# Cached values as one contiguous transfer, four keys in a row on a partition, and the turned probabilities with a stride of four

## The reference, cut to what matters

```python
q = _rope(_rmsnorm(q, q_norm_w), pos)
k = _rope(_rmsnorm(k, k_norm_w), pos)
kc = k_cache[block_table].reshape(bsz, L, HK, D)      # L = 512 cached keys
vc = v_cache[block_table].reshape(bsz, L, HK, D)
k_all = jnp.concatenate([kc, k], axis=1)              # 640 keys
v_all = jnp.concatenate([vc, v], axis=1)
...
scores = jnp.einsum('bqhd,bkhd->bhqk', q, k_all) * SCALE
scores = jnp.where(valid[:, None, None, :], scores, -1e+30)
probs = jax.nn.softmax(scores, axis=-1)
o = jnp.einsum('bhqk,bkhd->bqhd', probs, v_all)
return jnp.einsum('bse,de->bsd', o.reshape(bsz, seqlen, HQ * D), Wo)
```

## Time and profile before

| | us |
|---|---|
| median of 3 runs | 1304.53 (1304.43 to 1305.79) |
| the profiled execution, its own time | 1303.22 |
| its span, first to last instruction | 1301.4 |
| PE busy | 1252.7 (96%) |
| DVE busy | 984.4 (76%) |
| ACT busy | 835.0 (64%) |
| POOL busy | 830.8 (64%) |
| mean granted PE clock | 0.987 of full speed |

### The profile page before, as it was taken

How to read it: one execution, slowest core, us unless ns; L and a number is a source line. 1 busy time by engine, 2 the same in 40 slices (tenths; PEclk the granted TensorE clock), 3 DMA queues, 4 the chain that set the end, 5 groups by cost and what they waited for, 6 DMA issues and landing times. The chain is left out here.

```text
span 1301.4 us, 26180 instructions
## 1 busy us (share of the span) xinstructions
PE 1252.7 (96%) x7464; PEld 1067.8 (82%) x7464; DVE 984.4 (76%) x2380; ACT 835.0 (64%) x2501; POOL 830.8 (64%) x783
## 2 busy tenths in 40 slices
PE   5899998799999999999999999999999999999988
PEld 4666765588888888888888888888888888888878
DVE  3577757478878878888788788868888888888866
ACT  2677777466676666666766666666667666666731
POOL 1457557476767676668765876577667756775731
PEclk9899998899999999999999999999999999999999
DMA  8555553445555545555555555545555555555541
GB/s 288 214 200 205 203 211 130 111 117 139 137 139 141 140 133 149 131 140 141 151 130 141 138 140 128 144 126 139 131 140 143 137 142 142 135 138 137 137 130 66
DMA packets 288561, 191.48 MB, mean 147 GB/s; under 512 B 151201, under 2 KB 256674, under 8 KB 287266
## 3 DMA queue, kind: packets, MB, share of 16 engines
q1 hardware_dynamic: 287408, 189.64, 51.0%
q10 hardware_dynamic: 1010, 0.17, 0.1%
HBM read 143.60 MB, written 79.69 MB: 172 GB/s over the span
## 5 line engine op out<-in xcount | busy, mean ns | idle before, releaser
L1745 POOL TENSOR_TENSOR b_p_l<-b_moved,b_p_h 128x640 fp32r<-128x640 f32 x128 | 200.9, 1570 | 167.4 <-PE ps L1341 86.5
L1480 ACT ACTIVATE b_pf<-b_sm,b_mn 128x640 f32<-128x640 f32 x256 | 212.2, 829 | 128.0 <-DVE b_mn L1590 127.9
L1590 DVE CUSTOM_DVE_ANT_0 b_sm<-ps,mask_row,b_rstd 128x640 f32<-128x640 f32 x256 | 224.9, 878 | 51.8 <-PE ps L1267 46.5
L1492 ACT ACTIVATE b_p_h<-b_moved 128x640 fp32r<-128x640 f32 x128 | 94.6, 739 | 163.5 <-DMA b_moved<-blocks_of_probs 162.0
L1626 DVE SCALAR_TENSOR_TENSOR b_hacc<-ps,b_ri,b_hacc 128x512 f32<-128x512 f32 x248 | 182.4, 736 | 4.3 <-PE ps L1267 4.0
L1265 PE MATMUL ps<-b_w_h,x1t_h 128*128 128x512 f32 (+1 forms) x512 | 179.3, 350 | 0.1
L1265 PE MATMUL ps<-b_kt_h,b_qt_h 128*128 128x320 f32 x512 | 168.9, 330 | 6.0 <-DVE b_mn L1590 5.7
L1266 PE MATMUL ps<-b_w_l,x1t_h 128*128 128x512 f32 (+1 forms) x512 | 173.8, 340 | 0.0
L1267 PE MATMUL ps<-b_w_h,x1t_l 128*128 128x512 f32 (+1 forms) x512 | 173.6, 339 | 0.0
L1267 PE MATMUL ps<-b_kt_h,b_qt_l 128*128 128x320 f32 x512 | 158.9, 310 | 0.0
L1266 PE MATMUL ps<-b_kt_l,b_qt_h 128*128 128x320 f32 x512 | 158.7, 310 | 0.0
(11 more groups left out here) (170 smaller groups left out, 3344.6 us busy)
## 6 DMA issues: line engine op xcount, KB each, us to landing
blocks_of_probs<-b_blk SPq DMA_DIRECT2D x128, 320.0 KB, 2.5
b_moved<-blocks_of_probs SPq DMA_DIRECT2D x512, 80.0 KB, 2.0
kv_of_batch<-in_kv SPq DMA_DIRECT2D x128, 256.0 KB
b_ck<-kv_of_batch SPq DMA_DIRECT2D x64, 256.0 KB, 4.0
b_cv<-kv_of_batch SPq DMA_DIRECT2D x256, 64.0 KB, 1.9
raw<-in_w SPq DMA_DIRECT2D x32, 384.0 KB, 3.2
raw<-in_wo SPq DMA_DIRECT2D x32, 256.0 KB, 2.8
a_xt<-in_xt SPq DMA_DIRECT2D x8, 256.0 KB, 5.6
```

The lines of the kernel that those rows point to most:

```text
L1480: act.activation(pf[:, h % 2], sm[:, h % 2], ACT.Exp, bias=mn[:, m.b % 2, h:h + 1], scale=-1.0, accum_out=rs[:, m.b % 2, h:h + 1]).then_in ...
L1492: act.activation(blocks_of(p_h[:, :, h * P:(h + 1) * P]), moved[:, d].rearrange("p (a t j) -> p a t j", a=LT, j=QUAD), ACT.Copy).then_inc( ...
L1590: dve.tensor_tensor_reduce(sm[:, h % 2], score_row, mask_row[:, m.b], rstd[:, m.b % 4, h:h + 1], -MASKED, ALU.add, ALU.min, mn[:, m.b % 2, ...
L1745: pool.tensor_tensor(blocks_of(p_l[:, :, h * P:(h + 1) * P]), moved[:, d].rearrange("p (a t j) -> p a t j", a=LT, j=QUAD), blocks_of(p_h[: ...
```

## The change

The HBM buffer is laid out anew: for each sequence and head all keys of the 16 pages stand first and all values behind them, so that the 512 values of an item are one run of 256 KB. `value_rows` loads them in a single transfer: each partition takes four values in a row (2 KB), so partition p holds the keys 4p to 4p+3, key 4p+t in place t. Tile t of the values now has the keys t, t+4, t+8 and so on. The turned probabilities must follow. `turn_probs` loads as weights each fourth column of `pf` for the four tiles of cached keys, a step of 16 bytes in place of 4; the fifth tile, the new keys, stays as it was. `turn_blocks` becomes two instructions: one over the 512 cached columns, which reads with the same step, and one over the 128 new ones. ACT waits for 16 instead of 64 on the values' semaphore. The gather writes two runs of 16 KB for each head in place of one of 32 KB. Scores, mask, minima and exponents keep their order of keys.

```diff
@@ -83,7 +83,8 @@
                                                        min_val=0, max_val=PAGES - 1)
     for k in range(FOUR):
         n = first + k
-        sp.dma_start(kv_dram[n // NPP, :, n % NPP], t["kv"][bass.ds(four[k], 1)].rearrange("a g n -> (a g) n")).then_inc(gathered, 16)
+        page = t["kv"][bass.ds(four[k], 1)].rearrange("a g (k n) -> (a g) k n", k=2)
+        sp.dma_start(kv_dram[n // NPP, :, :, n % NPP], page).then_inc(gathered, 16)
 
 
 def phase1(nc, ctx, t, x1t_h, x1t_l, ident, consts, raw, raw_in, x1_dram, kv_dram, pages, gathered, ps):
@@ -1173,7 +1174,10 @@
             return ap.rearrange("p (c t j) -> p c t j", c=LT, j=QUAD)
 
         def by_tile(ap):
-            return ap.rearrange("p (t c j) -> p c t j", c=LT, j=QUAD)
+            return ap.rearrange("p (c j t) -> p c t j", c=LT, j=QUAD)
+
+        def by_rows(ap):
+            return ap.rearrange("p (c j) -> p c j", j=QUAD)
 
         def blocks_of(ap):
             return ap.rearrange("p t (a j) -> p a t j", a=LT)
@@ -1200,14 +1204,13 @@
                 if m.g == 0:
                     sp.wait_ge(gathered[m.b], 16 * NPP)
                 wait(sp, kcl_sb, m.n)
-                keys = kv_dram[m.b, m.g, :, 0:HD * PSIZE].rearrange("j (d s) -> d j s", d=HD)
+                keys = kv_dram[m.b, m.g, 0].rearrange("j (d s) -> d j s", d=HD)
                 sp.dma_start(ck[:].rearrange("p (j s) -> p j s", s=PSIZE), keys).then_inc(ck_in, 16)
             def value_rows(m):
 
                 wait(sp, vcl_sb, m.n)
-                for q in range(LT):
-                    rows_of = kv_dram[m.b, m.g, :, HD * PSIZE:].rearrange("(t q) (s d) -> q s t d", q=LT, d=HD)[q]
-                    sp.dma_start(cv[q * PSIZE:(q + 1) * PSIZE], rows_of).then_inc(cv_in, 16)
+                rows_of = kv_dram[m.b, m.g, 1].rearrange("j (p n) -> (j p) n", n=LT * HD)
+                sp.dma_start(cv[:].rearrange("p t d -> p (t d)"), rows_of).then_inc(cv_in, 16)
 
             def blocks_away(m, h):
 
@@ -1314,7 +1317,8 @@
                 pe.wait_ge(exp_sb, REP * m.n + h + 1)
                 wait(pe, pl_sb, len(BY_PE) * m.n + BY_PE.index(h))
                 for i in range(NT):
-                    mm = pe.transpose(turned_row[:, i], pf[:, h % 2, i * P:(i + 1) * P], ident[:])
+                    keys = pf[:, h % 2, L:] if i == LT else pf[:, h % 2, i:L:LT]
+                    mm = pe.transpose(turned_row[:, i], keys, ident[:])
                 mm.then_inc(pt_ps, 1)
 
             def value_pairs(m):
@@ -1457,7 +1461,7 @@
                 act.activation(kt_h[:, m.b % 2, L:], ps[:, PJK, 0:P], ACT.Copy).then_inc(knh_sb, 1)
 
             def cache_values(m):
-                act.wait_ge(cv_in, 16 * LT * (m.n + 1))
+                act.wait_ge(cv_in, 16 * (m.n + 1))
                 wait(act, pv_ps, m.n - 1)
                 act.activation(v_h[:, m.b % 2], cv[:], ACT.Copy).then_inc(vch_sb, 1)
 
@@ -1601,7 +1605,9 @@
                     dve.wait_ge(x1_out, 16 * B)
                 dve.wait_ge(exp_sb, REP * m.n + h + 1)
                 wait(dve, blk_out[d], 16 * m.n)
-                dve.transpose(by_quadrant(blk[:, d]), by_tile(pf[:, h % 2])).then_inc(blk_sb, 1)
+                blocks = by_quadrant(blk[:, d])
+                dve.transpose(blocks[:, :, 0:LT], by_tile(pf[:, h % 2, 0:L]))
+                dve.transpose(blocks[:, :, LT], by_rows(pf[:, h % 2, L:])).then_inc(blk_sb, 1)
 
             def low(m, h):
                 dve.wait_ge(ph_sb, len(BY_PE) * m.n + BY_PE.index(h) + 1)
@@ -1779,7 +1785,7 @@
 
 def build_program(nc, t, out):
     x1_dram = nc.dram_tensor("x1", [B, S, D], F32).ap()
-    kv_dram = nc.dram_tensor("kv_of_batch", [B, G, NPP, 2 * HD * PSIZE], F32).ap()
+    kv_dram = nc.dram_tensor("kv_of_batch", [B, G, 2, NPP, HD * PSIZE], F32).ap()
     with ExitStack() as ctx:
         sb = lambda n, s, d=F32: ctx.enter_context(nc.sbuf_tensor(n, s, d))
         ident = sb("ident", [P, P])
```

## The result

The changed kernel takes 1314.36 us (median of 6 runs, 1311.85 to 1315.94), against 1304.48 us for the kernel before (6 runs, 1297.11 to 1305.79): ratio 1.009, 95% interval 1.0067 to 1.0113. It is slower by about 10 us. The forecast was 1305.1 us, no change; the time lies at the far end of the wide range of 1302 to 1315, which was drawn to hold the rivals, and outside the forecast's own 1303 to 1307. The profiled execution took 1314.73 us, with a span of 1313.1 us; that of the kernel before was 1303.2 and 1301.4.

The account below looks back on a forecast made before the run. PE was taken to bound the kernel, busy 96% of the span. Transfers 0, PE's loads 0 and DVE 0.6 us on 1304.53 gave about 1305.1 us; own range 1303 to 1307, with rivals 1302 to 1315.

Parts of the forecast that it names:

- What bounds the kernel: Whole kernel: PE is busy 96% of the span, so longer PE instructions are paid in full.
- Transfers 0: Single values transfer and gather of 16 runs per page: no engine gets a new wait, 0 us.
- PE's transposes: 512 stepped weight loads in turn_probs: taken as hidden like contiguous loads of 128 columns, 0 us; bounds 0 to 72.
- My own lower price: PE's stepped loads in turn_probs: about 190 ns, spacing 0.11 to 0.12 us, 10 ns x 512 = 5.1 us.
- rival 2: PE's loads in turn_probs become the transposes' pace: +72 + 0.6, 1377 us; chance 0.09, including between 1 and 2.
- DVE's turning, +0.06: turn_blocks as two instructions, 0.82 us together: 0.06 us more each, step taken as free; upper end 0.62.
- rival 3: DVE's stepped read in turn_blocks at half pace: +6.2 us and up to tenths elsewhere, 1311 to 1315; chance 0.14.
- Who waits for it: Head 1's minima behind DVE's turning: ordinary slots hide it; slots without slack pay, 0.6 us, at most 6.2.
- this happens 10 times: Late and first slots: PE's load waits for DVE's minima 10 times per execution, 10 x 0.06 = 0.6 us.
- Rival 4: Late slots: turned blocks return from HBM sooner, shorter waits and less half clock: -4.3 us, 1300.3; chance 0.10.
- The sum: Whole kernel: transfers 0, PE's loads 0, DVE 0.6 us; 1304.53 + 0.6, about 1305.1 us.
- Rivals 1 and 3: Rival 1: PE's turn_probs loads slightly longer, +5.1 + 0.6, 1310.2 us, chance 0.12; rival 3: DVE's half-pace read, chance 0.14.

Follow-up runs that it names:

- the swap: On SP, head 1's blocks_back issued ahead of the next item's keys: kernel before 1295.17 us (ratio 0.9936), changed kernel 1305.32 us (1.0011).

## Why the prediction was wrong, step by step

- **What bounds the kernel**: right. PE is the bound; its longer instructions came through one to one.
- **Transfers 0**: right. Ratio 0.9977 with them alone, 0.9933 against 0.9936 with and without them.
- **PE's transposes, 0 taken from the row nearest by its columns**: wrong, mis-sized. The sum should have held 6.0 us. My own lower price (5.1, from loads of 190 ns at a spacing of 0.12) was the rival, and it is what happened: 209 ns, spacing 0.121. The row with the same number of columns was not the nearest one; it said how long a contiguous load hides, not what a stepped read takes. That the load was shorter than its matmul was no cover: PE's spacing grew by 12 ns though a load of 209 is still under a matmul of 283 (as the profile models it). Nor did the load become the pace, as rival 2 has it from about 190 ns on: 209 ns of load go with a spacing of 121. Between whole runs the 6.0 us show as 4.2 and 4.4, within their noise.
- **DVE's turning, +0.06**: the split was right (0.826), the step was mis-sized: 0.06 in the sum, 0.48 us in all measured, within the bounds of 0.06 and 0.62. It is not quite the half pace of rival 3: 1.93 ns for a column, where 1.09 doubled is 2.18.
- **Who waits for it**: right for ordinary slots (the slack held: 0.3 us left, no wait). Wrong in "this happens 10 times": the count was held fixed. Every turning that ends 0.48 later sends its blocks later, ACT waits 0.30 us more for each of them, and slots that were just in time became late: 19 waits for 10. The step from ACT's wait to a late slot is argued from the order of the work; what the runs show is that both go away with SP's order. So rival 3's 6.2 us, which was 10 x 0.62, was too small: without the swap DVE's part is 13. Its range of 1311 to 1315 holds the measured 1314.4, and the overall range reaches that far because of it. That is in part luck: the few us above 6.2 were meant for ordinary slots whose slack runs out, and in these the slack held; the rival has nothing for PE either.
- **Rival 4** named the wait behind the moved blocks and what it is worth (4.3 us), but not its cause. The single transfer of the values did not cure it, as the argument against it said (ACT's longest wait for the blocks is 5.6 us with both reads contiguous); SP's order did, for 8.6.
- **The sum** took both reads as hidden; neither was. Rivals 1 and 3 were priced as alternatives. They are two parts of one change, which both read with a step for one reason, and should have been one case: 1304.5 + 5.1 + 6.2 = 1315.8. Each had a chance of its own, and their joint outcome had none.

The Trainium skill, in "SBUF — State Buffer", section "Door 1: The DMA port swizzle", says that an access which starts a new line of 16 bytes is penalised, and that was the sentence against this change that I left without effect on the sum. At 16 bytes the runs agree: 209 ns for 140 on PE, 1.93 ns for 1.09 on DVE. At 8 bytes, where two elements still share a line, DVE pays nothing, as the rule has it, but PE's load pays in full, so that there the measurement decides against it.

## What to carry to other kernels

A read with a step is not free because its engine has room: on the engine that is the bound, 12 ns in each transpose became 6 us. Put a permutation where a run of 8 elements stays whole; here it cost nothing in the split of the keys, with the step of four moved into the layout of the inputs, and 10 to 13 us at the reads of the probabilities. And before a queue's order is taken as given, look for an issue that is ready, or soon will be, and stands behind one that isn't: that swap gave 8.6 us, where the new transfers gave nothing that can be told.

## What was not expected of the hardware

- A weight load of 128 columns of float32 took 139 to 141 ns contiguous and 201 to 209 ns at a step of 2, 3, 4 or 5 elements; transposes behind such loads followed each other each 117 to 121 ns, not each 109.
- DVE's 32 x 32 transposes took 1.09 ns for a column at steps 1 and 2, 1.42 at 3, 1.93 at 4 and 2.05 at 5.
- ACT and POOL read 512 columns permuted in runs of 8 elements, and wrote them in order, as fast as they read them in order (622 and 1284 ns, against 619 and 1297).
- One issue of 256 KB for the values took 0.34 us on SP where four of 64 KB took 1.73 to 2.40, and the time did not move: nothing waited for it.
